# Attention kernel: the top-32 mask added to the scores by GpSimd ahead of the exponential, probabilities and row sums written by ScalarE, one pipeline step more

## The chip, the cores and the metric

The kernel runs on one core of one Trainium2 chip. The metric is the device time of one execution in microseconds (us); lower is better. Five engines work side by side, each through its own queue in program order: TensorE (PE, with its weight loads shown apart as PEld), VectorE (DVE), ScalarE (ACT), GpSimd (POOL) and SyncE (SP, which here only issues transfers). They meet at semaphores.

## The reference

The input is 8 batches of 512 rows of 128 values. A layer of attention is followed by a mixture of experts, a small state-space mixer and the experts again; the change touches the attention alone. Cut to what matters:

```python
qkv = x @ Wqkv.T + bqkv                                 # 16 heads of 64
scores = einsum('bhid,bhjd->bhij', q, k) * SCALE
scores = scores + einsum('bhid,ijd->bhij', q, rel_k_emb[dist])
threshold = top_k(scores, 32)[0][..., -1:]              # the 32nd largest of a row of 512
scores = where(scores < threshold, -inf, scores)
attn = softmax(scores)
for i in range(3):                                      # ORDER = 3
    a_v = attn @ v_curr                                 # i == 0: + attn @ rel_v_emb[dist]
    v_curr = a_v
    res = res + sigmoid(alphas_raw[i]) * v_curr
out = res @ Wout.T + bout
```

## The kernel before, in words

`attention` handles two heads (a pair) of one batch at a time: 64 such iterations (`ITS`), each with 4 tiles of 128 rows (`NT`), so 256 tiles. A tile holds 2 heads x 512 scores on each of 128 partitions. All engines run the same sequence of slots, four in an iteration (`T` = 0 to 3). In one slot an engine works on several tiles of different age: `z.back(2)` is the tile that entered two slots ago, and `z.iteration(-2)` the pair two iterations back. The first and the last iterations are written out and those between are a loop whose body holds two iterations, 8 tiles. What runs when is the order in which `body` names it for each engine; nothing is scheduled automatically.

The way of a tile in the kernel before, all names as in the code:

- slot +0: TensorE makes the relative keys' products; ScalarE spreads them (`rel`), and two transfers through memory shift them into `relj`.
- slot +2: TensorE makes the scores in two banks, and ScalarE copies them into `sc` (a tensor of 2 buffers), three pieces for a head.
- slot +3: VectorE finds the 32 largest of each head's row by four rounds of `max` (8 values each) with `match_replace` between them (L846 to L867). ScalarE negates the row's maximum (`nmax`, L781) and takes the exponential of all 512 scores into `ex` (L788). For head 0 VectorE compares with the 32nd largest, multiplies and sums in one instruction (L875). For head 1 GpSimd compares (L952, into `kept`) and multiplies (L958).
- slot +4: SyncE sends the probabilities' band to memory, TensorE transposes them (L621) and ScalarE copies the transposes into `pt` (L757). ScalarE reads head 1's probabilities once more for their row sum (L825).
- slot +5: the band comes back shifted, ScalarE closes it (`band`, L703 to L716), TensorE turns it (L668), ScalarE keeps it (`band_t`, L797).

Two iterations back, the pair's values are multiplied by the probabilities three times. Each time TensorE multiplies (`mix`, L541), ScalarE copies (`mixed`, L694), TensorE transposes (L600), ScalarE copies (`raw`, L746), and GpSimd divides by the row sums (`u`, L916) and adds into `res` (L925, or L928 and L931). `mix` runs in slots 0, 1 and 2, and the copies and GpSimd's part in slots 1, 2 and 3.

Of the kernel before, what the change touches and what calls it, by code (L numbers as in the profile page):

```python
# [16 lines left out]
P = 128  # L17
B, N, D = 8, 512, 128
NT = N // P
# [9 lines left out]
SCALE = DH ** -0.5  # L29
HALF = MAXREL  # L30
# [354 lines left out]
def attention(nc, sem, sb, ps, k, t):  # L385
# [13 lines left out]
    s.maxes = sem("att_maxes")  # L399
    s.exps = sem("att_exps")  # L400
    s.probs = [sem(f"att_probs_of_head{h}") for h in range(2)]
    s.at_least = sem("att_at_least")
    s.row_sums = sem("att_row_sums")
# [59 lines left out]
    with nc.Block() as block:  # L463
        @block.sync
        def _(sp):
            def body(z, par):
# [14 lines left out]
                d, a = z.back(4), z.back(0)  # L481

                if d:
                    it, Td, n = d
                    qd = Td % 2
                    c0, c1 = known(sp, n + 1, 16 * (it * 2 + Td // 2))
                    for h in range(2):
                        sp.wait_ge(s.probs[h], c0)
# [41 lines left out]
        def _(pe):  # L530
            def body(z, par):
                T = z.T
                old, av, cur, nxt = z.iteration(-3), z.iteration(-2), z.iteration(0), z.iteration(1)
                def mix(it, values):

                    if not early(it * ORDER + T):
                        pe.wait_ge(s.mixed_kept, it * ORDER + T)
                    for jt in range(NT):
                        for h in range(2):
                            lhs = values[:, jt, h * DH:(h + 1) * DH] if T == 0 else values[:, jt, h, :]  # L540
                            last = nc.tensor.matmul(U[h * DH:(h + 1) * DH, :], lhs, pt[par][:, h, jt, :],  # L541
                                                    start=(jt == 0), stop=(jt == NT - 1 and T > 0))
                    return last


# [27 lines left out]
                if old is not None and T == 0:  # L573
                    pe.wait_ge(s.res_chain, old * 5 + 5)
                    if cur is not None:
                        pe.wait_ge(s.k_kept, cur + 1)
# [3 lines left out]
                    last.then_inc(s.res_turned, 1)  # L580

                if av is not None and T > 0:
                    pe.wait_ge(s.mixed_kept, av * ORDER + T)

                    if T == 1 and not early(av):
                        pe.wait_ge(s.out_added, av)
                    if T == 1 and cur is not None:
                        pe.wait_ge(s.k_kept, cur + 1)
                    if T == 2:
                        if cur is not None:  # L590
                            pe.wait_ge(s.v_kept, cur + 1)
                        else:
                            pe.wait_ge(s.raw_kept, av * ORDER + 1)
                    if T == 3:
                        if nxt is not None:
                            pe.wait_ge(s.q_kept, nxt + 1)
                        else:
                            pe.wait_ge(s.raw_kept, av * ORDER + 2)
                    for jt in range(NT):
                        last = nc.tensor.transpose(MISC[:, jt * P:(jt + 1) * P], mixed[:, jt * P:(jt + 1) * P],  # L600
                                                   k.ident[:, :])
                    last.then_inc(s.mixed_turned, 1)

                if av is not None and T == 0:
                    pe.wait_ge(s.probs_kept, (av + 1) * 2 * NT)
                    pe.wait_ge(s.v_ready, av + 1)
                    mix(av, v[par])

                d = z.back(4)
                if d:  # L610
                    it, Td, n = d
                    for h in range(2):
                        pe.wait_ge(s.probs[h], n + 1)
# [12 lines left out]
                if old is not None and T == 0:  # L626
# [7 lines left out]
                if T == 1 and cur is not None:  # L634
                    pe.wait_ge(s.k_kept, cur + 1)
                    if av is not None:
                        pe.wait_ge(s.raw_kept, av * ORDER + 1)
                    for jt in range(NT):
                        last = nc.tensor.matmul(MISC[:, jt * P:(jt + 1) * P], xt[par][:, jt * P:(jt + 1) * P],
                                                pj[par][:, J_WV:J_WV + P], start=True, stop=True)  # L640
                    last.then_inc(s.v_made, 1)

                if T == 2 and nxt is not None:
                    pe.wait_ge(s.pj_in[1 - par], 32 * (z.half(1) + 1))
                    if av is not None:
                        pe.wait_ge(s.raw_kept, av * ORDER + 2)
# [4 lines left out]
                if T == 3 and nxt is not None:  # L651
                    pe.wait_ge(s.q_kept, nxt + 1)
                    if av is not None:
                        pe.wait_ge(s.raw_kept, av * ORDER + 3)
# [3 lines left out]
                e = z.back(5)  # L658
# [12 lines left out]
                if av is not None and T in (1, 2):  # L671
                    pe.wait_ge(s.values_next, av * ORDER + T)
                    last = mix(av, u)
                    last.then_inc(s.mixed, 1)
                if av is not None and T == 0:
# [9 lines left out]
        def _(act):  # L685
            def body(z, par):
                T, sp2 = z.T, z.T % 2
                old, av, cur, nxt = z.iteration(-3), z.iteration(-2), z.iteration(0), z.iteration(1)

                if av is not None and T > 0:  # L690
                    act.wait_ge(s.mixed, av * ORDER + T)
                    if not early(av * ORDER + T - 1):
                        act.wait_ge(s.mixed_turned, av * ORDER + T - 1)
                    nc.scalar.activation(mixed[:, :], U[:, :], ACT.Copy).then_inc(s.mixed_kept, 1)  # L694

                e = z.back(5)
                if e:
# [3 lines left out]
                    act.wait_ge(s.row_sums, n + 1)  # L701
# [17 lines left out]
                if b:  # L719
# [3 lines left out]
                    act.wait_ge(s.rel_kept, n + 1)  # L723
                    for h in range(2):
                        act.wait_ge(s.scores_made, 2 * n + h + 1)
                        if not early(n - 1):
                            act.wait_ge(s.probs[h], n - 1)
                        last = nc.scalar.activation(sc[q][:, h, lo:hi], SC[h][:, lo:hi], ACT.Copy)  # L728
                        if lo > 0:
                            last = nc.scalar.activation(sc[q][:, h, 0:lo], SC[h][:, 0:lo], ACT.Identity,  # L730
                                                        bias=rel[q][:, h, 0:1])
                        if hi < N:
                            last = nc.scalar.activation(sc[q][:, h, hi:N], SC[h][:, hi:N], ACT.Identity,
# [3 lines left out]
                if old is not None and T == 0:  # L737
# [4 lines left out]
                if av is not None and T > 0:  # L742
                    act.wait_ge(s.mixed_turned, av * ORDER + T)
                    if not early(av * ORDER + T - 1):
                        act.wait_ge(s.values_next, av * ORDER + T - 1)
# [3 lines left out]
                d = z.back(4)  # L749
                if d:  # L750
                    it, Td, n = d
                    dpar = 1 - par
# [23 lines left out]
                c = z.back(3)  # L776
                if c:
                    it, Tc, n = c
                    q = Tc % 2
                    act.wait_ge(s.tops, 2 * n + 2)  # L780
                    nc.scalar.activation(nmax[q][:, :], top[q][:, :, 0], ACT.Copy, scale=-1.0).then_inc(s.maxes, 1)  # L781
                    act.wait_ge(s.maxes, n + 1)
                    for h in range(2):
                        if not early(n - 1):
# [1146 lines left out]
```

## Time and profile before

| what | value |
|---|---|
| median of 3 runs | 3345.88 us (3342.76 to 3358.94) |
| span of the profiled execution, first to last instruction | 3382.6 us |
| VectorE (DVE) busy | 2933.7 us, 87% |
| TensorE (PE) busy | 2884.2 us, 85% |
| ScalarE (ACT) busy | 2463.6 us, 73% |
| GpSimd (POOL) busy | 1642.2 us, 49% |

The profile is of one execution. The only time that it gives for that execution is its span, 3382.6 us, 36.7 us or 1.1% over the median of the timed runs. Shares are of the whole span, of which attention's tiles fill about 69 us to 2660 us.

### The profile page before, as it was taken

The numbers are of one execution on the slowest core, as the hardware profiler recorded it, in microseconds if no ns is written. First come the engines' busy times: TensorE is split into PE (matmuls) and PEld (weight loads), VectorE is DVE, ScalarE is ACT, GpSimd is POOL, SyncE is SP. The second block draws the span as 40 slices with busy tenths as digits, with TensorE's granted clock in tenths as the row PEclk, the third lists the DMA queues.
The fourth block names the chain that finished last, engine by engine and source line by source line (L and its number), as shares of the span: only waits on it lengthen the run. The fifth ranks groups of instructions, "written<-read, shape, count | busy, mean of one in ns | idle before, by whom it ended". The sixth has DMA issues, their size and how long they took to land. (4 is left out here: it accounts for less than half of the span.)

```text
span 3382.6 us, 62340 instructions
## 1 busy us (share of the span) xinstructions
PE 2884.2 (85%) x13152; PEld 1671.5 (49%) x13152; DVE 2933.7 (87%) x6964; ACT 2463.6 (73%) x7615; POOL 1642.2 (49%) x1196
## 2 busy tenths in 40 slices
PE   4799889998889889988888998898888677888958
PEld 2454444454444445444444444444444344677743
DVE  5999999999999999999999999999999556676546
ACT  3888888888888888888888888888888523332214
POOL 1455555555555555555555555555555424222104
PEclk7999999999999999999999999999999867677659
DMA  4444444444444444444444444444444100000001
GB/s 124 135 133 126 136 130 130 130 132 126 132 129 136 127 134 129 130 134 132 132 132 130 132 132 134 132 134 126 134 130 127 48 17 10 16 7 4 0 7 45
DMA packets 293411, 356.42 MB, mean 105 GB/s; under 512 B 24850, under 2 KB 239956, under 8 KB 293204
## 3 DMA queue, kind: packets, MB, share of 16 engines
q1 hardware_dynamic: 291076, 351.66, 35.3%
q10 hardware_dynamic: 2128, 2.85, 0.3%
q14 instruction: 182, 1.49, 0.1%
q8 instruction: 25, 0.41, 0.1%
HBM read 140.00 MB, written 169.87 MB: 92 GB/s over the span
## 5 line engine op out<-in xcount | busy, mean ns | idle before, releaser
L855 DVE MAX8 top<-work 128x8 f32<-128x512 f32 x1536 | 978.5, 677 | 0.0
L952 POOL TENSOR_SCALAR kept<-scores,top 128x512 f32<-128x512 f32 x256 | 489.9, 1914 | 540.0 <-DVE top L855 535.5
L865 DVE MATCH_REPLACE8 work<-top,work 128x512 f32<-128x512 f32 x1024 | 682.7, 673 | 0.0
L556 PE MATMUL bank<-keys_of_head,qt 128*128 128x512 f32 x1024 | 598.2, 669 | 0.0
L541 PE MATMUL bank<-probs_t,u 128*64 128x512 f32 x2048 | 467.7, 599 | 4.0 <-POOL u L916 3.6
L852 DVE MAX8 top<-scores 128x8 f32<-128x512 f32 x512 | 327.4, 679 | 99.8 <-issue 83.9
L916 POOL TENSOR_TENSOR u<-raw,inverse 128x512 f32<-128x512 f32 x192 | 200.2, 1043 | 433.1 <-ACT raw L746 433.1
L958 POOL TENSOR_TENSOR probs_of_tile<-kept,exps 128x512 f32<-128x512 f32 x256 | 326.6, 1276 | 61.1 <-POOL kept L952 53.7
L560 PEld LDWEIGHTS bank<-relj,identity 128*128 128x128 f32 x1024 | 210.4, 206 | 285.7 <-issue 276.9
L788 ACT ACTIVATE exps<-scores,nmax 128x512 f32<-128x512 f32 x512 | 341.7, 714 | 8.3
L865 DVE MATCH_REPLACE8 work<-top,scores 128x512 f32<-128x512 f32 x512 | 341.3, 673 | 0.0
L621 PE MATMUL bank<-identity,probs_of_tile 128*128 128x128 f32 x2048 | 280.3, 276 | 25.7 <-POOL probs_of_tile L958 20.4
L560 PE MATMUL bank<-relj,identity 128*128 128x256 f32 (+1 forms) x1024 | 291.2, 368 | 7.2 <-DMA relj<-rel_scratch 7.2
L757 ACT ACTIVATE probs_t<-bank 128x512 f32<-128x512 f32 x512 | 284.1, 626 | 1.6 <-PE bank L621 1.6
L728 ACT ACTIVATE scores<-bank 128x192 f32<-128x192 f32 (+1 forms) x512 | 180.7, 353 | 132.8 <-POOL probs_of_tile L958 88.9
L621 PEld LDWEIGHTS bank<-identity,probs_of_tile 128*128 128x128 f32 x2048 | 227.9, 141 | 89.6 <-issue 63.7
L556 PEld LDWEIGHTS bank<-keys_of_head,qt 128*128 128x128 f32 x1024 | 186.8, 206 | 169.8 <-issue 163.3
L541 PEld LDWEIGHTS bank<-probs_t,u 128*64 128x64 f32 x2048 | 135.7, 137 | 245.0 <-issue 220.4
L875 DVE SCALAR_TENSOR_TENSOR probs_of_tile<-scores,top,exps 128x512 f32<-128x512 f32 x256 | 233.5, 912 | 9.5 <-DVE top L855 4.7
L541 PE MATMUL bank<-probs_t,v 128*64 128x512 f32 x1024 | 235.4, 602 | 0.0
L703 ACT ACTIVATE band<-band 128x129 f32<-128x129 f32 x512 | 155.5, 304 | 100.3 <-DMA band<-probs_scratch 96.0
L694 ACT ACTIVATE mixed<-bank 128x512 f32<-128x512 f32 x192 | 114.6, 597 | 116.3 <-PE bank L541 68.4
(259 smaller groups left out, 5594.2 us busy)
## 6 DMA issues: line engine op xcount, KB each, us to landing
rel_scratch<-rel SPq DMA_DIRECT2D x256, 383.0 KB, 3.8
relj<-rel_scratch SPq DMA_DIRECT2D x256, 256.0 KB, 2.8
probs_scratch<-probs_of_tile SPq DMA_DIRECT2D x256, 256.0 KB, 2.5
band<-probs_scratch SPq DMA_DIRECT2D x256, 256.0 KB, 3.6
pair_j<-table_j SPq DMA_DIRECT2D x64, 257.0 KB, 2.9
xt<-stream_normed_t SPq DMA_DIRECT2D x64, 256.0 KB, 3.0
pair_o<-table_o SPq DMA_DIRECT2D x64, 67.0 KB, 2.4
experts_xs<-stream_normed_t SPq DMA_DIRECT2D x16, 256.0 KB, 2.3
```

What stands on the lines that cost most here:

```text
L541: last = nc.tensor.matmul(U[h * DH:(h + 1) * DH, :], lhs, pt[par][:, h, jt, :], start=(jt == 0), stop=(jt == NT - 1 and T > 0))
L556: nc.tensor.matmul(SC[h][:, :], qt[bpar][:, Tb * P:(Tb + 1) * P], t.kz[bpar][h][:, :], start=True, stop=False)
L560: nc.tensor.matmul(SC[h][:, lo:hi], k.ident[:, :], relj[q][:, h, at:at + hi - lo], start=False, stop=True).then_inc(s.scores_made, 1)
L621: last = nc.tensor.transpose(PT[h][:, jt * P:(jt + 1) * P], t.prob[Td][:, h, HALF + jt * P:HALF + (jt + 1) * P], k.ident[:, :])
L757: nc.scalar.activation(pt[dpar][:, h, :, Td * P:(Td + 1) * P], PT[h][:, :].rearrange("p (j i) -> p j i", j=NT), ACT.Copy).then_inc(s.probs ...
L788: nc.scalar.activation(ex[q][:, h, :], sc[q][:, h, :], ACT.Exp, bias=nmax[q][:, h:h + 1]).then_inc(s.exps, 1)
L852: nc.vector.max(top[q][:, h, 0:8], sc[q][:, h, :]).then_inc(s.tops, 1)
L855: nc.vector.max(top[q][:, h, 8 * r:8 * r + 8], work[:, h, :]).then_inc(s.next_tops, 1)
L865: nc.vector.match_replace(out=work[:, h, :], in_to_replace=top[q][:, h, 8 * r:8 * r + 8], in_values=sc[q][:, h, :] if r == 0 else work[:, ...
L875: nc.vector.scalar_tensor_tensor(out=t.prob[Tc][:, 0, HALF:HALF + N], in0=sc[q][:, 0, :], scalar=top[q][:, 0, TOPK - 1:TOPK], in1=ex[q][:, ...
L952: nc.gpsimd.tensor_scalar(kept[:, :], sc[q][:, 1, :], top[q][:, 1, TOPK - 1:TOPK], None, ALU.is_ge).then_inc(s.at_least, 1)
L958: nc.gpsimd.tensor_tensor(t.prob[Tc][:, 1, HALF:HALF + N], kept[:, :], ex[q][:, 1, :], ALU.mult).then_inc(s.probs[1], 1)
```

## The change: what it does

1. GpSimd gets the whole mask. For each tile it negates the maximum and the 32nd value of both heads in one small instruction (`neg`), and then, for each of the two heads: adds minus the 32nd value and multiplies by 2^100 (one instruction), takes the minimum with 0 and the maximum with -3e38 (one instruction; so 0 for a score that stays and a huge negative value for one that goes), and adds this to the scores in place.
2. ScalarE's exponential reads the masked scores, writes the probabilities themselves, and sums each row with the same instruction. `nmax`, `ex`, `kept`, VectorE's L875, GpSimd's L952 and L958 and ScalarE's L781 and L825 are gone.
3. The exponential moves to slot +4. The probabilities' transfer and transposes move to slot +5, the band to slot +6. The three multiplications of the values move to slots 1, 2 and 3, the third one's copies to slot 0 of the next iteration, the values' projection `v` from slot 1 to slot 0, and the output's projection from slot 0 to slot 1.
4. The scores have 4 buffers, in place of 2.

The core of the diff:

```diff
-    sc = two("scores", [P, 2, N])
+    sc = [sb(f"scores{T}", [P, 2, N]) for T in range(NT)]
...
-    nmax = two("nmax", [P, 2])
-    ex = two("exps", [P, 2, N])
-    kept = sb("kept", [P, N])
+    neg = two("minus_max_and_least", [P, 2, 2])
+    cut = sb("cut", [P, 2, N])
...
+                    if not early(n - 3):
+                        act.wait_ge(s.probs, 2 * n - 6)
                     for h in range(2):
                         act.wait_ge(s.scores_made, 2 * n + h + 1)
-                        if not early(n - 1):
-                            act.wait_ge(s.probs[h], n - 1)
...
-                c = z.back(3)
-                if c:
-                    it, Tc, n = c
-                    q = Tc % 2
-                    act.wait_ge(s.tops, 2 * n + 2)
-                    nc.scalar.activation(nmax[q][:, :], top[q][:, :, 0], ACT.Copy, scale=-1.0).then_inc(s.maxes, 1)
...
+                x = z.back(4)
+                if x:
+                    it, Tx, n = x
+                    xpar, q = 1 - par, Tx % 2
...
+                        act.wait_ge(s.masked, 2 * n + h + 1)
+                        nc.scalar.activation(t.prob[Tx][:, h, HALF:HALF + N], sc[Tx][:, h, :], ACT.Exp,
+                                             bias=neg[q][:, h, 0:1],
+                                             accum_out=rs[xpar][:, 2 * Tx + h:2 * Tx + h + 1]).then_inc(s.probs, 1)
...
-                    act.wait_ge(s.probs[1], n + 1)
-                    nc.scalar.activation(ex[Td % 2][:, 1, :], t.prob[Td][:, 1, HALF:HALF + N], ACT.Copy,
-                                         accum_out=rs[dpar][:, 2 * Td + 1:2 * Td + 2]).then_inc(s.row_sums, 1)
...
+                    if not early(n - 1):
+                        dve.wait_ge(s.negated, n - 1)
...
-                    nc.vector.scalar_tensor_tensor(out=t.prob[Tc][:, 0, HALF:HALF + N], in0=sc[q][:, 0, :],
-                                                   scalar=top[q][:, 0, TOPK - 1:TOPK], in1=ex[q][:, 0, :],
-                                                   op0=ALU.is_ge, op1=ALU.mult,
-                                                   accum_out=rs[cpar][:, 2 * Tc:2 * Tc + 1]).then_inc(s.probs[0], 1)
...
-                    nc.gpsimd.tensor_scalar(kept[:, :], sc[q][:, 1, :], top[q][:, 1, TOPK - 1:TOPK], None,
-                                            ALU.is_ge).then_inc(s.at_least, 1)
...
-                    nc.gpsimd.tensor_tensor(t.prob[Tc][:, 1, HALF:HALF + N], kept[:, :], ex[q][:, 1, :],
-                                            ALU.mult).then_inc(s.probs[1], 1)
+                    nc.gpsimd.tensor_scalar(neg[q][:, :, :], ends, -1.0, 0.0, ALU.mult, ALU.add).then_inc(s.negated, 1)
...
+                    for h in range(2):
+                        nc.gpsimd.tensor_scalar(cut[:, h, :], sc[Tc][:, h, :], neg[q][:, h, 1:2], STEEP,
+                                                ALU.add, ALU.mult).then_inc(s.compared, 1)
...
+                        nc.gpsimd.tensor_scalar(cut[:, h, :], cut[:, h, :], 0.0, NEG,
+                                                ALU.min, ALU.max).then_inc(s.cut, 1)
...
+                        nc.gpsimd.tensor_tensor(sc[Tc][:, h, :], sc[Tc][:, h, :], cut[:, h, :],
+                                                ALU.add).then_inc(s.masked, 1)
```

What this does to the order of GpSimd's instructions, in the loop's body. First a slot 2 of the kernel before: `u`, `tmp` and `res` are the values' part, `kept` and `probs_of_tile` the mask of head 1. (REGISTER_ALU and ISA rows work out what a semaphore is compared with.)

```order
L909 REGISTER_ALU
L915 REGISTER_ALU
L916 TENSOR_TENSOR u<-raw,inverse 128x512
L928 TENSOR_TENSOR tmp<-u,pair_o 128x512
L930 REGISTER_ALU
L931 TENSOR_TENSOR res<-res,tmp 128x512
L365 ISA
L952 TENSOR_SCALAR kept<-scores,top 128x512
L954 REGISTER_ALU
L955 ISA
L958 TENSOR_TENSOR probs_of_tile<-kept,exps 128x512
```

The same work after the change, now in slot 3: the mask is seven instructions of both heads, six of them over 512 values on each partition.

```order
L893 REGISTER_ALU
L899 REGISTER_ALU
L900 TENSOR_TENSOR u<-raw,inverse 128x512
L912 TENSOR_TENSOR tmp<-u,pair_o 128x512
L914 REGISTER_ALU
L915 TENSOR_TENSOR res<-res,tmp 128x512
L366 ISA x2
L940 TENSOR_SCALAR minus_max_and_least<-top 128x4
L946 TENSOR_SCALAR cut<-scores,minus_max_and_least 128x512 x2
L951 TENSOR_SCALAR cut<-cut 128x512 x2
L955 TENSOR_TENSOR scores<-scores,cut 128x512 x2
```

What moved: the two instructions of the mask became seven, and the part with `u` stands ahead of them as before.

## Rows read from the trace of the kernel before

**Rows 1.** Busy time of each engine in two stretches of attention.

```profile
core 0: us, PE busy (x) PEld busy (x) DVE busy (x) ACT busy (x) POOL busy (x), PEclk, DMA share, GB/s
300.00:2500.00 2200.00, 1961.83 (x9100) 1067.66 (x9102) 2113.50 (x4877) 1909.03 (x6016) 1238.23 (x923) 0.97 0.45 131
```

**Rows 2.** Waits of VectorE from 300 to 2500 us: total, times, longest.

```profile
DVE top L852 <- issue: 80.7, 27, 3.5
DVE probs_of_tile L875 <- DVE top L855: 2.8, 17, 0.2
```

**Rows 3.** Timeline of VectorE, one loop body of 8 tiles: start, us, engine.

```profile
1015.19 1.29 DVE L852 MAX8 top<-scores 128x8 f32<-128x512 f32 x2 [3.03 <-issue]
...
1023.92 0.73 DVE L875 SCALAR_TENSOR_TENSOR probs_of_tile<-scores,top,exps 128x512 f32<-128x512 f32 x1
...
1025.25 1.27 DVE L852 MAX8 top<-scores 128x8 f32<-128x512 f32 x2
...
1082.07 1.49 DVE L875 SCALAR_TENSOR_TENSOR probs_of_tile<-scores,top,exps 128x512 f32<-128x512 f32 x1 [0.17 <-DVE top L855]
...
1083.49 1.28 DVE L852 MAX8 top<-scores 128x8 f32<-128x512 f32 x2
...
1096.89 0.69 DVE L852 MAX8 top<-scores 128x8 f32<-128x512 f32 x1 [3.37 <-issue]
```

**Rows 4.** Groups of VectorE: count, busy us, mean ns.

```profile
L875 DVE SCALAR_TENSOR_TENSOR probs_of_tile<-scores,top,exps 128x512 f32<-128x512 f32 x256 | 233.5, 912 | 9.5 <-DVE top L855 4.7 <-ACT exps L788 3.0
```

**Rows 5.** Groups of GpSimd, shapes kept apart.

```profile
L952 POOL TENSOR_SCALAR kept<-scores,top 128x512 f32<-128x512 f32 x256 | 489.9, 1914 | 540.0 <-DVE top L855 535.5 <-issue 4.0
L958 POOL TENSOR_TENSOR probs_of_tile<-kept,exps 128x512 f32<-128x512 f32 x256 | 326.6, 1276 | 61.1 <-POOL kept L952 53.7 <-ACT band L712 5.4
L916 POOL TENSOR_TENSOR u<-raw,inverse 128x512 f32<-128x512 f32 x192 | 200.2, 1043 | 433.1 <-ACT raw L746 433.1
L931 POOL TENSOR_TENSOR res<-res,tmp 128x512 f32<-128x512 f32 x128 | 163.3, 1276 | 10.0
...
L938 POOL TENSOR_TENSOR v<-vraw,pair_j 128x512 f32<-128x512 f32 x64 | 83.7, 1308 | 131.1 <-ACT vraw L805 131.1
...
L220 POOL MEMSET zeros<- 128x256 f32 x1 | 0.3, 312 | 0.3 <-POOLq L1920 0.3
L226 POOL TENSOR_SCALAR_AFFINE_SELECT anti_identity<-anti_identity 128x128 f32<-128x128 f32 x1 | 0.3, 293 | 0.0
...
L221 POOL MEMSET identity<- 128x128 f32 x1 | 0.2, 205 | 0.0
```

**Rows 6.** Timeline of GpSimd around one tile's mask and the values' part.

```profile
1073.68 1.28 POOL L938 TENSOR_TENSOR v<-vraw,pair_j 128x512 f32<-128x512 f32 x1 [1.76 <-ACT vraw L805]
1074.93 1.56 POOL L952 TENSOR_SCALAR kept<-scores,top 128x512 f32<-128x512 f32 x1
1076.74 1.27 POOL L958 TENSOR_TENSOR probs_of_tile<-kept,exps 128x512 f32<-128x512 f32 x1 [0.24 <-POOL kept L952]
1079.50 1.04 POOL L916 TENSOR_TENSOR u<-raw,inverse 128x512 f32<-128x512 f32 x1 [1.49 <-ACT raw L746]
1080.62 1.04 POOL L928 TENSOR_TENSOR tmp<-u,pair_o 128x512 f32<-128x512 f32 x1
1081.74 1.27 POOL L931 TENSOR_TENSOR res<-res,tmp 128x512 f32<-128x512 f32 x1
1082.99 2.00 POOL L952 TENSOR_SCALAR kept<-scores,top 128x512 f32<-128x512 f32 x1
```

**Rows 7.** Groups of ScalarE, 300 to 2500 us.

```profile
L825 ACT ACTIVATE exps<-probs_of_tile 128x512 f32<-128x512 f32 x216 | 134.8, 624 | 1.3
...
L825 ACT ACTIVATION_READ_ACCUMULATOR exps<-probs_of_tile 128x1 f32 x216 | 41.5, 192 | 0.0
...
L781 ACT ACTIVATE nmax<-top 128x2 f32<-128x2 f32 x217 | 60.3, 278 | 0.0
```

**Rows 8.** Timeline, all engines: the values' chain from one multiplication to the next.

```profile
1030.35 3.65 PE L541 MATMUL bank<-probs_t,u 128*64 128x512 f32 x16
...
1034.06 0.60 ACT L694 ACTIVATE mixed<-bank 128x512 f32<-128x512 f32 x1 [0.51 <-PE bank L541]
...
1037.88 0.33 ACT L728 ACTIVATE scores<-bank 128x192 f32<-128x192 f32 x1 [0.89 <-POOL probs_of_tile L958]
...
1038.51 0.60 ACT L746 ACTIVATE raw<-bank 128x512 f32<-128x512 f32 x1
...
1039.27 1.04 POOL L916 TENSOR_TENSOR u<-raw,inverse 128x512 f32<-128x512 f32 x1 [1.49 <-ACT raw L746]
...
1040.50 1.08 PE L541 MATMUL bank<-probs_t,u 128*64 128x512 f32 x4
```

**Rows 9.** Waits of TensorE and ScalarE from 300 to 2500 us.

```profile
PE bank L678 <- ACT band_t L797: 111.6, 54, 2.1
...
ACT scores L728 <- POOL probs_of_tile L958: 81.0, 81, 2.0
```

More of the change, by code:

```diff
@@ L29 @@
 SCALE = DH ** -0.5
+STEEP = 2.0 ** 100
 HALF = MAXREL
@@ L398, in attention @@
     s.tops = sem("att_tops")
[L399 to L403, printed above, removed]
+    s.negated = sem("att_negated")
+    s.compared = sem("att_compared")
+    s.cut = sem("att_cut")
+    s.masked = sem("att_masked")
+    s.probs = sem("att_probs")
     s.probs_turned = sem("att_probs_turned")
@@ L624, in body @@
                         last.then_inc(s.probs_turned, 1)
-                if old is not None and T == 0:
+                if T == 0 and cur is not None:
+                    pe.wait_ge(s.k_kept, cur + 1)
+                    if old is not None:
+                        pe.wait_ge(s.raw_kept, old * ORDER + 3)
+                    for jt in range(NT):
+                        last = nc.tensor.matmul(MISC[:, jt * P:(jt + 1) * P], xt[par][:, jt * P:(jt + 1) * P],
+                                                pj[par][:, J_WV:J_WV + P], start=True, stop=True)
+                    last.then_inc(s.v_made, 1)
+                if T == 1 and old is not None:
                     pe.wait_ge(s.res_kept, old + 1)
@@ L632, in body @@
                     last.then_inc(s.out_made, 1)
[L634 to L641, printed above, removed]
                 if T == 2 and nxt is not None:
@@ L669, in body @@
                     last.then_inc(s.band_turned, 1)
[L671 to L675, printed above, removed]
+                if av is not None and T in (2, 3):
+                    pe.wait_ge(s.values_next, av * ORDER + T - 1)
+                    mix(av, T - 1, u).then_inc(s.mixed, 1)
+                if av is not None and T == 1:
                     pe.wait_ge(s.band_kept, (av + 1) * NT)
@@ L688, in body @@
                 old, av, cur, nxt = z.iteration(-3), z.iteration(-2), z.iteration(0), z.iteration(1)
[L690 to L693, printed above, removed]
+                turning, step = (old, 3) if T == 0 else (av, T - 1)
+                if turning is not None and step > 0:
+                    act.wait_ge(s.mixed, turning * ORDER + step)
+                    if not early(turning * ORDER + step - 1):
+                        act.wait_ge(s.mixed_turned, turning * ORDER + step - 1)
                     nc.scalar.activation(mixed[:, :], U[:, :], ACT.Copy).then_inc(s.mixed_kept, 1)
-                e = z.back(5)
+                e = z.back(6)
                 if e:
@@ L885, in body @@
                     nc.vector.reciprocal(inv[par][:, :], rs[par][:, :]).then_inc(s.inverse, 1)
-                if old is not None and T == 0:
+                if old is not None and T == 1:
                     dve.wait_ge(s.out_made, old + 1)
@@ L952, in body @@
[L952 to L959 removed]
+                        pool.wait_ge(s.probs, used)
@@ new lines, in body @@
+                    ends = bass.AP(top[q][:, :, :].tensor, top[q][:, :, :].offset,
+                                   [list(top[q][:, :, :].ap[0]), [TOPK, 2], [TOPK - 1, 2]])
+                    nc.gpsimd.tensor_scalar(neg[q][:, :, :], ends, -1.0, 0.0, ALU.mult, ALU.add).then_inc(s.negated, 1)
+                    met()
+                    pool.wait_ge(s.negated, turned_over)
+                    if not early(before):
+                        pool.wait_ge(s.masked, before)
+                    for h in range(2):
+                        nc.gpsimd.tensor_scalar(cut[:, h, :], sc[Tc][:, h, :], neg[q][:, h, 1:2], STEEP,
+                                                ALU.add, ALU.mult).then_inc(s.compared, 1)
```

180 lines of the change are left out of this document (84 added, 96 removed).

## The prediction

> **What bounds the kernel now.** I read the windows first. From 300 to 2500 us, all attention, VectorE is busy 2113.5 of 2200 us, 96%; TensorE 89%, ScalarE 87%, GpSimd 56% [rows 1]. The next view is who VectorE waits for: almost nobody. Its idle time is 80.7 us in 27 pieces put down to "issue" [rows 2]. The timeline shows one such piece at each turn of the loop, 3.03 and 3.37 us, between the last tile of one body and the first of the next [rows 3]. So VectorE sets the pace: one body of 8 tiles lasts 1096.89 - 1015.19 = 81.70 us [rows 3], 10.21 us a tile, 40.85 us an iteration. The whole of attention is 64 iterations of that.
>
> In that body a tile's search takes 8.73 us (1015.19 to 1023.92) [rows 3], and behind it comes L875, the masked product for head 0. L875 has two prices. It lasts 0.73 us at 1023.92 and 1.49 us at 1082.07 [rows 3], where GpSimd was adding into `res` (1081.74 to 1083.01) when it began [rows 6]. Its mean is 912 ns over 256 [rows 4]. The two exclude each other for a while. After the change VectorE's per-tile work is `max` and `match_replace` alone; two `max` take 1.27 to 1.29 us wherever they stand [rows 3], also at 1083.49, beside L952 on GpSimd [rows 6]. So I charge no contention.
>
> **The change on VectorE.** It loses L875: 256 x 0.912 = 233 us [rows 4], and in the sampled body the 7 us that are left of its 81.70 when what VectorE keeps is taken off. It keeps the search (8 x 8.74), the reciprocal and the add into the stream of each iteration (1025.25 - 1023.92 = 1.33 us less L875's 0.66 [rows 3], so 0.67 twice), and the 3.3 us at the loop's turn: 69.9 + 1.3 + 3.3 = 74.6 us, 37.3 an iteration. Its new wait, for `negated` two tiles back, has a whole tile's slack; behind it stands only its own next search. If VectorE stays the bound the gain is (40.85 - 37.3) x 64 = 227 us.
>
> **The change on ScalarE.** Per tile it loses L781 (0.28 us) and L825 (0.62 us and an accumulator read of 0.19, which overlaps its neighbours) and gains two accumulator reads of 0.19 at most [rows 7]: 0.5 to 0.7 us less a tile. From 8.8 us busy a tile (1909 us over 2200 at 10.14 us a tile [rows 1]) it falls to about 8.2, under VectorE's 9.3. The four score buffers take away its wait for the mask of the tile two back, 81.0 us in 81 waits [rows 9].
>
> **TensorE** does the same work in another order. What paces it is a chain: `mix` starts at 1030.35, ScalarE copies at 1034.06, copies `raw` at 1038.51 after a wait of 0.89 us for the score buffer, GpSimd makes `u` at 1039.27, and the next `mix` starts at 1040.50 [rows 8]. That is 10.15 us for a slot, and 9.26 without the 0.89. Two slots of an iteration have it. The other two take 40.85 - 2 x 10.15 = 20.55 us today, with a stall of 2.1 us at L678 in them, 54 times [rows 9]; I take 1.2 us off, since less ScalarE work will stand ahead of `band_t`, and get 19.3. This estimate from those rows gives 2 x 9.3 + 19.3 = 37.9, with some jitter 38.3 us an iteration. It lies a little over VectorE's 37.3. The one step more is one slot at the end: +5 to +9 us once.
>
> **The change on GpSimd**, which decides. The part that it keeps costs, from starts in the timeline: `u`, `tmp`, `res` 1079.50 to 1082.99 = 3.49 us, twice an iteration; `u` with the first `res` 2.3; `v` 1073.68 to 1074.93 = 1.25 [rows 6]. Sum 10.6 us an iteration. It loses the mask of head 1, and gains for each tile:
> - one small negation and a handover to itself: 0.1 plus 0.24 (the gap at 1076.74 [rows 6]);
> - two adds of two tensors: 2 x 1.27 = 2.55 (the same form as L958 and L931, 1276 ns [rows 5]);
> - four `tensor_scalar` over 512 values with arithmetic, each x plus 0.08 of gap (1080.62 + 1.04 to 1081.74 [rows 6]).
>
> That is 3.2 + 4x a tile, so 23.5 + 16x an iteration, and at most 1.5 more if a turn of the loop costs GpSimd the 3 us that it costs VectorE. For x = 0.77 this gives 35.8 to 37.3; it ties with VectorE at x = 0.86 (0.77 with the turn), and with today's 40.85 at x = 1.08 (0.99).
>
> No row shows x: the trace has no arithmetic `tensor_scalar` on GpSimd. Bounds: below, a memset. 256 columns take 312 ns and 128 take 205 [rows 5], 0.84 ns a column, so 512 take 0.53 us. Above, L952, one comparison over 512 values. Its mean is 1914 ns [rows 5], but it starts beside L875 nearly always; where it doesn't, at 1074.93, it takes 1.56 us [rows 6]. Between: two-input products where one input is a broadcast take 1.04 us (L916 and L928), which read one tensor more than a `tensor_scalar`; and the affine select of 128 columns takes 293 ns, which with the fixed part of the memset (205 - 107 = 98 ns) is 1.5 ns a column, 0.88 us for 512. A comparison must make a 0 or a 1 of a condition and is the dearest of these per value; a two-tensor product is below it at 1.27 us though it reads twice. I take x = 0.8, by the affine select and a little under the broadcast product, with 0.53 to 1.56 as its range.
>
> Two rules of the Trainium skill, "GPSIMD Engine Reference", stand beside this. Section 3.1 has a tight loop over 512 elements at 769 ns, and says that bodies which produce a condition cost about twice those that don't; by that x would be 0.77 and an iteration of GpSimd 35.8 us. Against the change speaks section 4.1: elementwise work belongs on VectorE, GpSimd being about twice as slow with two inputs. The trace agrees with the second as far as it shows it (1.27 us against L875's 0.73).
>
> With x = 0.8 GpSimd needs 36.3 to 37.8 us an iteration, TensorE's chain 38.3, VectorE 37.3. Three engines within 2 us of each other seldom meet the best of them, so I take 38.5: (38.5 - 40.85) x 64 = -150 us, +6 for the extra slot. Against the profiled 3382.6 that is 3239; the median of the runs stands 36.7 below that span, and taken off it the forecast is **3202 us**. Its own range is 3115 to 3320: VectorE's bound with nothing lost (-227), up to x = 1.0.
>
> **Rivals.**
> 1. GpSimd becomes the bound at a price like the broadcast product with two operations, x about 1.05 to 1.3. An iteration is then 40.3 to 44.3 us and up to 1.5 more: 0 to +315 us, centre +130, 3480 us. For it: two operations in an instruction, and nothing in the trace that shows the second to be free. The rule of section 4.1 above, taken for one input too, would end here. Against: the affine select. It ends slower, and decides from x = 1.08 on. Chance 0.22.
> 2. All arithmetic costs like the comparison, x = 1.43 to 1.56: 46.4 to 48.5 us an iteration, and 1.5 more with the turn: +355 to +585, about 3815 us. For it: the only `tensor_scalar` in the trace over 512 values. Against: it alone has a condition. Chance 0.15.
> 3. The mask is cheap, but the values' chain or the waits at L678 keep the old pace: `mix` to `mix` stays at 10.15 us because ScalarE's order, not the buffer, fixes `raw`. Then 40.85 us an iteration, within 20 us of before. Against: 0.89 us of it is plainly the score buffer [rows 8]. Chance 0.07.
>
> The forecast keeps 0.56.
>
> **How the numbers follow.** A change of 0.5%, 17 us, is about what a measurement of this kernel can tell from none. Faster: the forecast's 0.56 and a little of rival 1's and 3's lower edges, 0.58. Same: 0.08. Slower: 0.34. The range runs from 3115 (VectorE's own bound) to 3600, x about 1.28: above it lies rival 2 and the tail of rival 1, some 0.17.
>
> **What the profile after would show.** `cut` rows on GpSimd near 0.8 us each (rival 1: over 1.05; rival 2: 1.4 and more). No L875, and VectorE's `max` waiting a little for ScalarE's scores or for `negated` instead of never. ScalarE without waits for the score buffer. `mix` to `mix` in two slots near 9.3 us. If x is right and the time is not, look for ScalarE waiting at the exponential for `masked`, and TensorE at the band. If GpSimd is the bound, it is busy over 95%, and VectorE waits for `negated`.

## The result, and the profile after

The changed kernel takes 3400.6 us (median of 4 runs, 3399.5 to 3404.1), the kernel before 3348.5 us beside it. The ratio is 1.017, 95% interval 1.014 to 1.020: slower by 52 us, where the prediction said 3202 us and faster. The page of the changed kernel, its span, busy times and clock:

```profile
span 3398.5 us, 62039 instructions
...
PE 2871.5 (84%) x13152; PEld 1666.5 (49%) x13152; DVE 2738.2 (81%) x6452; ACT 2286.3 (67%) x7359; POOL 2167.6 (64%) x2476
...
PEclk7999999999999999999999999999999968676659
```

VectorE lost 195 us of work and ScalarE 177, and GpSimd gained 525. So the work went where it was meant to go, and no engine is full: in attention VectorE fell from 96% busy [rows 1] to 88% (1934.5 of 2200 us in the row below), GpSimd is at 76%. The same stretch of the changed kernel:

```profile
300.00:2500.00 2200.00, 1942.85 (x9037) 1064.15 (x9037) 1934.49 (x4412) 1742.83 (x5747) 1669.90 (x1991) 0.96 0.44 130
```

How long an iteration lasts on the average is read from VectorE's reciprocal, once an iteration: the first and the last start, divided by 63. Before and after:

```profile
L885 DVE RECIPROCAL inverse<-row_sums x64: 189/197/203, 126.9 to 2666.2; 128x8 f32<-128x8 f32 x64
```

```profile
L862 DVE RECIPROCAL inverse<-row_sums x64: 176/183/203, 122.0 to 2683.8; 128x8 f32<-128x8 f32 x64
```

That is 40.31 us before and 40.66 after. What took the place of VectorE's work is in the waits of the changed kernel from 300 to 2500 us (total, times, longest):

```profile
POOL v L922 <- PE bank L676: 270.4, 53, 5.7
...
DVE stream L869 <- PE bank L638: 180.6, 53, 4.0
POOL u L900 <- ACT raw L744: 143.7, 108, 3.1
ACT band L701 <- DMA band<-probs_scratch: 137.3, 126, 2.5
...
PE bank L676 <- ACT band_t L794: 107.0, 53, 2.0
PE bank L541 <- POOL u L900: 91.5, 54, 2.6
```

The rows of `v`, of `stream` and the last are new: in the kernel before, `v` waited for ScalarE's copy (92.9 us in the same stretch), VectorE's addition into `stream` did not wait, and TensorE waited 3.6 us for `u` in the whole span. The output's products and the addition that reads them both moved from slot 0 to slot 1; why the addition now waits 3.4 us an iteration was not taken apart, but the experiments below tell whether it sets the pace. The last row can be followed in the timeline of all engines, one iteration's slots 1 and 2:

```profile
990.38 1.08 PE L676 MATMUL bank<-band_t,rel_values 128*64 128x512 f32 x4 [2.02 <-ACT band_t L794]
...
991.55 1.27 POOL L922 TENSOR_TENSOR v<-vraw,pair_j 128x512 f32<-128x512 f32 x1 [4.70 <-PE bank L676]
...
992.90 0.20 POOL L940 TENSOR_SCALAR minus_max_and_least<-top 128x4 f32<-128x4 f32 x1
...
994.93 0.60 ACT L744 ACTIVATE raw<-bank 128x512 f32<-128x512 f32 x1
995.98 2.51 POOL L955 TENSOR_TENSOR scores<-scores,cut 128x512 f32<-128x512 f32 x2
...
998.44 1.05 POOL L900 TENSOR_TENSOR u<-raw,inverse 128x512 f32<-128x512 f32 x1
...
999.54 5.35 PE L541 MATMUL bank<-probs_t,u 128*64 128x512 f32 x16 [2.56 <-POOL u L900]
```

GpSimd is about to write `v` for the next pair. The buffer is the one that `mix` of step 0 reads, and its release is the semaphore `mixed`, which TensorE raises only after L676, the last product of slot 1. Before the change that product stood in slot 0, a slot ahead of `v`; now both are in slot 1. GpSimd waits 4.70 us, with slot 1's mask and slot 2's `u` queued behind. `raw` is there at 995.53 (994.93 + 0.60), but `u` starts at 998.44, and TensorE waits 2.56 us. What that wait costs on top is seen in L541: 5.35 us for 16 products, where before it was 3.65 [rows 8]. The granted clock goes with it. Two windows of the changed kernel at that place: behind each stretch's length stand the busy times of TensorE, its weight loads, VectorE, ScalarE and GpSimd, then the granted clock:

```profile
996.00:999.50 3.50, 0.99 (x4) 0.28 (x2) 3.50 (x7) 3.12 (x10) 3.49 (x4) 1.00 0.41 116
...
1001.00:1003.00 2.00, 2.00 (x8) 0.53 (x6) 2.00 (x6) 0.00 (x0) 1.77 (x3) 0.50 0.23 41
```

TensorE was busy for 0.99 of the 3.5 us from 996 to 999.5, at full clock (2.4 GHz). From 1001 to 1003 us it was busy all the time, at 0.50, the lower of its two levels (1.2 GHz).

This is the longer of two kinds of iteration that take turns. From 300 to 2500 us TensorE waited 26 times for about 2.55 us and 28 times for 0.9 to 1.2 us, and 21 of the 26 long waits were followed by 16 products in 5.0 to 5.35 us. Nor is the lower level new. The kernel before shows it too, here behind a stall of 2.06 us at L678 that ended at 1021.69:

```profile
1023.00:1026.00 3.00, 3.00 (x6) 1.45 (x6) 3.00 (x8) 2.10 (x9) 1.84 (x1) 0.50 0.40 110
```

The means from 300 to 2500 us are 0.97 before [rows 1] and 0.96 after, so the lower level by itself does not explain the loss.

GpSimd's prices, the unknown of the prediction, came out on its cheap side. Groups of GpSimd in the changed kernel:

```profile
L955 POOL TENSOR_TENSOR scores<-scores,cut 128x512 f32<-128x512 f32 x512 | 643.4, 1279 | 0.0
L946 POOL TENSOR_SCALAR cut<-scores,minus_max_and_least 128x512 f32<-128x512 f32 x512 | 354.3, 692 | 65.3 <-issue 40.8 <-POOL minus_max_and_least L940 0.2
L951 POOL TENSOR_SCALAR cut<-cut 128x512 f32<-128x512 f32 x512 | 305.8, 613 | 21.5
```

### The profile page after: what moved, and what is told of

Its sections match the earlier page's. It is cut to its first block and busy times, and to the rows that moved or that the text cites. A ratio compares the mean times of both kernels' runs of the same rounds, so it can differ in the third digit from the quotient of the medians.

```text
span 3398.5 us, 62039 instructions
## 1 busy us (share of the span) xinstructions
PE 2871.5 (84%) x13152; PEld 1666.5 (49%) x13152; DVE 2738.2 (81%) x6452; ACT 2286.3 (67%) x7359; POOL 2167.6 (64%) x2476
## 5 line engine op out<-in xcount | busy, mean ns | idle before, releaser
L955 POOL TENSOR_TENSOR scores<-scores,cut 128x512 f32<-128x512 f32 x512 | 643.4, 1279 | 0.0
L541 PE MATMUL bank<-probs_t,u 128*64 128x512 f32 x2048 | 508.4, 642 | 112.6 <-POOL u L900 112.5
L841 DVE MAX8 top<-scores 128x8 f32<-128x512 f32 x512 | 339.6, 684 | 112.5 <-ACT scores L731 101.9
L946 POOL TENSOR_SCALAR cut<-scores,minus_max_and_least 128x512 f32<-128x512 f32 x512 | 354.3, 692 | 65.3 <-issue 40.8
L784 ACT ACTIVATE probs_of_tile<-scores,minus_max_and_least 128x512 f32<-128x512 f32 x512 | 378.6, 773 | 21.8 <-POOL scores L955 21.2
L541 PEld LDWEIGHTS bank<-probs_t,u 128*64 128x64 f32 x2048 | 145.7, 147 | 388.5 <-issue 250.2
L951 POOL TENSOR_SCALAR cut<-cut 128x512 f32<-128x512 f32 x512 | 305.8, 613 | 21.5
L922 POOL TENSOR_TENSOR v<-vraw,pair_j 128x512 f32<-128x512 f32 x64 | 81.3, 1270 | 336.6 <-PE bank L676 315.6
L620 PE MATMUL bank<-identity,probs_of_tile 128*128 128x128 f32 x2048 | 270.0, 275 | 8.3 <-ACT probs_of_tile L784 4.4
L869 DVE TENSOR_TENSOR stream<-bank,stream 128x512 f32 (+1 forms) x64 | 44.3, 692 | 253.0 <-PE bank L638 253.0
```

The source lines that it names most:

```text
L620: last = nc.tensor.transpose(PT[h][:, jt * P:(jt + 1) * P], t.prob[Td][:, h, HALF + jt * P:HALF + (jt + 1) * P], k.ident[:, :])
L784: nc.scalar.activation(t.prob[Tx][:, h, HALF:HALF + N], sc[Tx][:, h, :], ACT.Exp, bias=neg[q][:, h, 0:1], accum_out=rs[xpar][:, 2 * Tx + h ...
L841: nc.vector.max(top[q][:, h, 0:8], sc[Tc][:, h, :]).then_inc(s.tops, 1)
L946: nc.gpsimd.tensor_scalar(cut[:, h, :], sc[Tc][:, h, :], neg[q][:, h, 1:2], STEEP, ALU.add, ALU.mult).then_inc(s.compared, 1)
L951: nc.gpsimd.tensor_scalar(cut[:, h, :], cut[:, h, :], 0.0, NEG, ALU.min, ALU.max).then_inc(s.cut, 1)
L955: nc.gpsimd.tensor_tensor(sc[Tc][:, h, :], sc[Tc][:, h, :], cut[:, h, :], ALU.add).then_inc(s.masked, 1)
```

## The experiments

All times are medians with the ratio to the kernel before, run on the same chip, since the kernel before itself lies between 3342 and 3359 us from chip to chip. Differences to the changed kernel are of medians and carry that spread: the first four gains below are 107, 111, 90 and 173 us so, and 129, 123, 108 and 193 us by the ratios. Theory 1 is the new wait just told. Its rivals are that GpSimd's amount of work, or VectorE's, or the longer pipeline holds the kernel.

**v behind the mask.** In GpSimd's body the block of `v` moves from ahead of the mask to behind it.

```diff
-                if T == 1 and cur is not None:
-                    pool.wait_ge(s.v_kept, cur + 1)
...
                         nc.gpsimd.tensor_tensor(sc[Tc][:, h, :], sc[Tc][:, h, :], cut[:, h, :],
                                                 ALU.add).then_inc(s.masked, 1)
+                if T == 1 and cur is not None:
+                    pool.wait_ge(s.v_kept, cur + 1)
```

> The changed kernel, with GpSimd's addition for the values of the next pair (v) moved behind the mask of the same slot; nothing else. Theory 1 (the new wait): in the changed kernel v waits 5.1 us once an iteration for the end of the multiplication by the old v (L676), the mask and u stand behind it, TensorE then waits 2.6 us for u and runs the next products at a lower clock. Then this edit gives back 2 to 3 us an iteration, 130 to 200 us: 3200 to 3270 us, and the wait at L541 for u falls from 91 us (300 to 2500 us) to under 20. Rival (GpSimd's added work itself, or the longer pipeline): the wait is only where slack shows, and the time stays within 0.5% of 3400 us.

Measured: 3293.8 us, ratio 0.979 (0.974 to 0.983). 107 us come back from this order alone, short of the 130 to 200 that were expected. The row of TensorE's wait for `u`, 91.5 us in the changed kernel, is gone from its waits; of the weight loads' wait for it 17.9 us are left in 107 waits.

**v released by its own semaphore.** `v` stays ahead of the mask.

```diff
-                    mix(av, 0, v[par])
+                    mix(av, 0, v[par]).then_inc(s.v_read, 1)
...
-                    if not early((cur - 2) * ORDER + 1):
-                        pool.wait_ge(s.mixed, (cur - 2) * ORDER + 1)
+                    if not early(cur - 1):
+                        pool.wait_ge(s.v_read, cur - 1)
```

> The changed kernel, v left ahead of the mask, but released by a semaphore of its own when the first multiplication (which is all that reads v) has ended, instead of by the end of L676. Theory 1: as the run before, 3200 to 3270 us, since the multiplication ends at 1027.7 us in the trace and GpSimd is free at 1028.8. If the order on GpSimd matters and not the wait, this one stays at 3400 us while the run before gains.

Measured: 3289.4 us, ratio 0.980 (0.976 to 0.985), the same as the run before, and 19 us short of the expected range as well: what matters is that `v` does not hold up what stands behind it, not where it stands. The timeline of this kernel shows `v` right behind the mask of slot 0, without a wait, four microseconds before the start of the product that it used to wait for:

```profile
1025.00 1.28 POOL L923 TENSOR_TENSOR v<-vraw,pair_j 128x512 f32<-128x512 f32 x1
...
1028.99 1.08 PE L677 MATMUL bank<-band_t,rel_values 128*64 128x512 f32 x4 [2.02 <-ACT band_t L795]
...
1034.58 1.04 POOL L901 TENSOR_TENSOR u<-raw,inverse 128x512 f32<-128x512 f32 x1 [2.62 <-ACT raw L745]
...
1035.81 3.65 PE L542 MATMUL bank<-probs_t,u 128*64 128x512 f32 x16
```

Now GpSimd waits for `raw`, and the next `mix` starts 0.19 us after `u` has ended and takes 3.65 us at full clock. The stall of 2.02 us at L677 (L676 of the changed kernel) stands unchanged.

**The band's copy first.** In slot 1 ScalarE's L794 goes ahead of the two exponentials.

```diff
+                if e and T == 1:
+                    it, Te, n = e
...
+                                         ACT.Copy).then_inc(s.band_kept, 1)
                 x = z.back(4)
                 if x:
...
-                if e:
+                if e and T != 1:
```

> The changed kernel, with ScalarE's copy of the band (L794) in slot 1 moved ahead of the two exponentials of that slot. The wait of TensorE at L676 (2.0 us, once an iteration) should fall to about 0.6 and v be released 1.4 us earlier. Theory 1: TensorE's stalls set the pace, so 1.4 to 3 us an iteration, 3210 to 3310 us. Rival: no change, within 0.5% of 3400 us.

Measured: 3310.9 us, ratio 0.985 (0.981 to 0.988), 90 us faster than the changed kernel and 1 us outside the slow edge of what was expected. Two waits of this kernel, from 300 to 2400 us:

```profile
POOL v L932 <- PE bank L676: 194.9, 52, 4.2
...
PE bank L676 <- ACT band_t L780: 32.0, 52, 0.6
```

TensorE's stall fell from 2.0 to 0.6 us, and GpSimd's wait for `v` from 5.1 to 3.7, by the same 1.4.

**Both edits** (own semaphore, band's copy first).

> Both edits: v released by its own semaphore, and the band's copy ahead of the exponentials in slot 1. Theory 1: TensorE then needs about 36 us an iteration and VectorE's 37.3 is the bound: 3180 to 3210 us. Rival: 3400 us, or no better than the better of the two single edits because another engine holds at 38 us.

Measured: 3227.6 us, ratio 0.960 (0.956 to 0.963). This is 173 us under the changed kernel and 4% under the kernel before; the single edits gave 111 and 90. It is not quite the 3180 to 3210 that VectorE's bound would have given. The longer pipeline is all in this kernel, so it is not what made the changed kernel slow. The page and the windows (300 to 2400 us; 1.00 is the granted clock):

```profile
span 3230.6 us, 62097 instructions
...
PE 2795.1 (87%) x13152; PEld 1635.6 (51%) x13152; DVE 2715.0 (84%) x6452; ACT 2260.0 (70%) x7359; POOL 2167.0 (67%) x2476
```

```profile
300.00:2400.00 2100.00, 1917.28 (x9251) 1059.96 (x9250) 1959.20 (x4513) 1763.09 (x5895) 1708.58 (x2037) 1.00 0.47 140
```

The clock went from 0.96 to 1.00 with no edit to TensorE's work: in this stretch the mean rounds to full clock. Each repair by itself gave 0.97 and 0.98. An iteration lasts 38.0 us by VectorE's reciprocal, of which VectorE is busy 35.5 (1959.2 / 2100 of it). Its waits show what is next:

```profile
ACT band L702 <- DMA band<-probs_scratch: 243.0, 179, 2.7
...
DVE stream L880 <- PE bank L639: 139.5, 55, 3.4
```

**The kernel before, band's copy first.** The same edit to the kernel before, in slot 0.

```diff
+                if e and T == 0:
...
                 c = z.back(3)
                 if c:
...
-                if e:
+                if e and T != 0:
```

> The kernel before, with the same edit to it as gave 90 us in the changed one: ScalarE's copy of the band (L797) in slot 0 ahead of that slot's exponentials. Theory 1: before was held by VectorE, so taking 1.4 us of TensorE's stall away buys nothing, within 0.5% of the kernel before. Rival (TensorE's stalls held the kernel before as well): 60 to 120 us faster.

Measured: 3341.2 against 3341.6 us, ratio 0.999 (0.997 to 1.001). What is worth 90 us in the changed kernel is worth nothing in the kernel before, though the same stall fell from 2.1 us [rows 9] to 0.6 (32.1 us in 52 waits). In part another wait took its place: TensorE's waits for GpSimd's probabilities at L621 grew from 10 to 34 us (300 to 2500 us).

**Less work for VectorE**, in the kernel before and in the changed one. The last round of the search reads half a row, so the threshold of both is another one.

```diff
-                                nc.vector.max(top[q][:, h, 8 * r:8 * r + 8], work[:, h, :]).then_inc(s.next_tops, 1)
+                                nc.vector.max(top[q][:, h, 8 * r:8 * r + 8], work[:, h, 0:N // 2 if r == 3 else N]).then_inc(s.next_tops, 1)
```

> The kernel before, with the last round of the search (values 25 to 32) looking at the first 256 of 512 scores only, so its threshold is another one: 0.55 to 0.7 us less VectorE work a tile, with every wait kept. Theory 1 (VectorE is the bound of the kernel before): 120 to 175 us faster. If TensorE's chain is the true bound: under 40 us.

> The changed kernel with the same shorter last round. Theory 1 (VectorE no longer sets the pace there): within 1% of 3400 us, at most 35 us faster. If VectorE still is the bound: 120 to 175 us faster.

Measured: the kernel before 3327.1 us, ratio 0.996 (0.992 to 0.999); the changed kernel 3398.7 us, ratio 1.018 (1.015 to 1.021), against 1.017 without the edit. The second is as expected: VectorE has no part in the changed kernel's time. The first misses theory 1 and falls where its rival stood, under 40 us. Two of these `max` take 0.54 us less a tile together (409 against 676 ns each), 138 us in all, and 14 came out. The groups of VectorE's L875 show one place where the rest went, and the waits another:

```profile
L875 DVE SCALAR_TENSOR_TENSOR probs_of_tile<-scores,top,exps 128x512 f32<-128x512 f32 x256 | 271.1, 1059 | 61.3 <-ACT exps L788 35.9 <-DVE top L855 21.6 <-issue 2.4
```

L875 grew from 912 to 1059 ns [rows 4], 38 us in all. It now lies beside GpSimd's instructions for longer, 0.94 us of overlap on the average against 0.74, and 96 of the 256 take over 1.2 us against 55. Its wait for ScalarE's exponential grew from 3.0 to 35.9 us. So VectorE in the kernel before was busy 96% of the time and still did not hold it alone; something else, which these two runs do not name, was only some 14 us behind.

**Both in the kernel before**, band's copy first and the shorter round.

> The kernel before with both of its single edits: ScalarE's band copy first in slot 0, and the shorter last round of VectorE's search. Alone each gave under 0.5%. Theory 2 (two bounds that lie within 15 us of each other, VectorE's work and TensorE's chain with its stall): together they give clearly more than the sum, 50 to 120 us faster than the kernel before. Rival (a third chain holds it, such as the score buffers): again under 20 us.

Measured: 3322.5 us, ratio 0.989 (0.987 to 0.991), 36 us. That is twice the sum of the two (0.1% and 0.4%), but neither the 50 us of theory 2 nor under the 20 of its rival. TensorE's stall is a part of the second bound and not the whole. What else holds it wasn't settled; ScalarE still waits for the score buffers there (66.6 us in 68 waits). The kernel before with four score buffers was not tried.

**Less work for GpSimd.** The two clamping instructions of a tile are left out, and the factor is 1, so that the mask is no mask; first in the changed kernel.

```diff
-STEEP = 2.0 ** 100
+STEEP = 1.0
...
-                        nc.gpsimd.tensor_scalar(cut[:, h, :], cut[:, h, :], 0.0, NEG,
-                                                ALU.min, ALU.max).then_inc(s.cut, 1)
```

> The changed kernel with GpSimd's two clamping instructions of each tile left out (and the factor 2^100 set to 1, so the mask is no mask): 1.2 us less GpSimd work a tile. Theory 1: GpSimd's amount of work is not the bound, but in slot 1 its mask stands between v and u, so u comes 1.2 us sooner once an iteration and a part of the 2.6 us at L541 goes: 1.2 to 2 us an iteration, 75 to 130 us faster. Rival (GpSimd's load is the bound): 4 x 1.2 us an iteration, 300 us, down to what the next engine allows at 37.3 us an iteration, 3190 us. Rival (it has no part in it): no change.

Measured: 3297.8 us, ratio 0.987 (0.984 to 0.989), 103 us faster than the changed kernel. This is inside what theory 1 gave, but by itself it would also suit a weaker form of the rival. Its waits from 300 to 2500 us are those of theory 1. GpSimd did not use the time that it saved but waited longer for `v`, and TensorE's wait for `u` went from 91.5 us to 16.9 (total, times, longest):

```profile
POOL v L922 <- PE bank L676: 384.4, 55, 7.8
...
PE bank L541 <- POOL u L900: 16.9, 21, 1.1
```

The same edit on top of both repairs tells them apart:

> The kernel with both edits, and GpSimd's two clamping instructions of each tile left out (factor 1 in place of 2^100, so the mask is no mask). In the changed kernel leaving them out gave 100 us. Theory 1: that was the mask standing between the late v and u, so with v released in time it gives nothing, within 0.5% of 3228 us. Rival (GpSimd's amount of work is a bound in its own right): 50 us or more faster.

Measured: 3223.2 us, ratio 0.963 (0.961 to 0.965), against 0.960 for both repairs alone. 1.2 us less a tile on GpSimd is worth 100 us while the late `v` pushes the mask in front of `u`, and nothing when it doesn't. GpSimd's amount of work is no bound in either kernel: in the changed one it stands idle before `v`, and in the repaired one less of it changes nothing.

**What holds the repaired kernel.** Two more on top of both repairs. In one VectorE's addition into the stream, which waits for TensorE's output products, moves behind the first round of slot 2's tile:

```diff
-                if old is not None and T == 1:
-                    dve.wait_ge(s.out_made, old + 1)
...
+                        if T == 2 and r == 0:
+                            into_stream()
```

> The kernel with both edits (v's own semaphore, the band's copy first in slot 1), and VectorE's addition into the stream moved from behind slot 1's tile to behind the first round of slot 2's tile. VectorE waits there 2.5 to 3.4 us once an iteration for the output's products. If VectorE's 37.3 us are the bound of that kernel (38.0 us an iteration), this gives 10 to 40 us. If TensorE's and ScalarE's chain holds it, no change within 0.5% of 3228 us.

> The kernel with both edits and the shorter last round of VectorE's search. If VectorE is the bound of that kernel at 3228 us, 100 us or more faster; if TensorE's and ScalarE's chain is, within 0.5% of it; between, both are near.

Measured: 3217.3 us, ratio 0.957 (0.955 to 0.959), for the first, and 3223.2 us, ratio 0.959 (0.956 to 0.961), for the second. Neither is told apart from 0.960 (0.956 to 0.963). The first says little by itself, since 10 us faster is both the low end of what VectorE's bound would give and inside the 0.5%. In it the wait for the output's products is gone, and VectorE waits for ScalarE's scores in its place (104 us from 300 to 2400 us). The second decides, where 100 us or more would have come: VectorE is not the bound at 38.0 us an iteration either. By what is left that is the chain through ScalarE, TensorE and the band's transfer; it was not tested by itself.

## Why the prediction was wrong, step by step

**GpSimd's price, "I take x = 0.8": right in kind, about a fifth too dear.** The arithmetic instructions take 0.69 and 0.61 us, less than half of the comparison's 1.56 [rows 6]. The affine select and the broadcast product, the nearest rows, both lay over it. One mask takes 5.6 us (1000.69 to 1006.29 in the trace of the changed kernel), where 3.2 + 4 x 0.8 = 6.4 was forecast. Rivals 1 and 2 fall with that: the kernel became slower without either of them. Of the Trainium skill, "GPSIMD Engine Reference", the 769 ns of section 3.1 for a tight loop over 512 values was nearer than 0.8 and still over both measured prices. The rule on bodies that produce a condition stands in its section 7 and not in 3.1; here the comparison costs 2.3 to 2.5 times the arithmetic. The row of section 4.1 that the prediction quotes calls only operations with two inputs twice as slow, and those with one input roughly line-rate; 0.69 and 0.61 us, beside 0.64 for VectorE's `max` over as many values [rows 3], agree, so that row spoke against rival 1 and not for it.

**What VectorE and ScalarE lose: right.** VectorE's busy time fell by 195 us (L875's 233 us are gone, and the rest grew a little), and ScalarE's by 0.7 us a tile (177 us / 256), as stated. No contention was forecast for `max` and `match_replace`, and `match_replace` takes 675 ns after as 673 before, `max` 679 as 677.

**The step that failed stands under the change on GpSimd: "the part that it keeps costs ... `v` 1.25".** It was charged as work and never as a wait. The prediction went through the waits that the diff adds (`negated`, `masked`), but not through those whose text is the same and whose other end has moved. The line `pool.wait_ge(s.mixed, (cur - 2) * ORDER + 1)` is in both kernels. TensorE's signal for it moved from slot 0 to slot 1, and `v` stayed in slot 1. The runs showed in its place a wait of 5.1 us once an iteration (270.4 us in 53 waits), and behind it TensorE's for the late `u` (91.5 us in 54 waits). The two runs on `v` show what it costs: 107 and 111 us.

**The values' chain, "9.26 without the 0.89": too short, because a wait took the place of the one removed.** In the kernel with `v` repaired, `mix` to `mix` is 1045.78 - 1035.81 = 9.97 us, with both repairs 9.80. ScalarE no longer waits for a score buffer, but from 300 to 2400 us it waits longer for the band's transfer: 70.1 us in 139 waits before, 243.0 in 179 with both repairs. That this is what holds `raw` back is argued from the order of ScalarE's work and was not tested. This is rival 3 in part. "Two slots of an iteration have it" was misread as well. Of the three intervals between the starts of an iteration's multiplications only the one from step 1 to step 2 is like that (medians from 300 to 2400 us before: 16.6, 10.15 and 14.2); with both repairs they are 15.0, 9.8 and 13.0, so most of what was gained lies in the other two.

**"I take 1.2 us off" the stall at L678: wrong.** It stayed at 2.0 us (107.0 us in 53 waits). ScalarE's copy still stood behind both exponentials, and taking `nmax` away did not bring it forward. Moving it did, and was worth 62 us with `v` repaired (3289 to 3228).

**"VectorE sets the pace": half right.** Shortening its work by 138 us in the kernel before gave 14. A second bound lay close behind, which the busy share of 96% can't show. Its 37.3 us for the time after were too many as well. The 3.3 us at the loop's turn are no row in the waits of the changed or the repaired kernel, and VectorE is busy only 35.5 us an iteration there; why they are gone was not tested.

**The baseline, "(38.5 - 40.85) x 64 = -150 us": some 55 us too much.** The sampled body of 40.85 us was longer than the mean of its own trace, 40.31: 35 us. And that execution was a long one. Taking 36.7 off brings the sum to the median of the runs, but the gain that it is added to was still counted against the long execution. The kernel before with the band's copy first, which takes as long as the kernel before (ratio 0.999), has 39.98 us an iteration in a trace of 3344.0 us: 21 us more. Against 39.98 the same working gives -95 us and a forecast near 3257 us, an estimate. By spans the change costs 16 us, by medians 52.

**Small slips.** GpSimd's kept part adds to 10.5 us, not 10.6; L875 is put in with 0.66 us where its row has 0.73; the lower end of the range, 3382.6 - 227 - 36.7, is 3119, not 3115. None of them moves the forecast.

Together: of the 198 us between 3202 and 3400.6, the late `v` is 111 and the stall at L676 62, when they are repaired in this order (90 for the stall's repair and 83 for the other, in the reverse order). The 26 that are left come close to the baseline, some 55 us too low, less the 31 us by which 38.0 us an iteration is under the forecast's 38.5. So with both waits gone the forecast's pace was met and a little more, but its parts were not the ones named.

## What to carry to other kernels

When a stage moves by a slot, list every semaphore that it raises, and look at who waits for it, also in lines that the diff leaves alone: a signal that moves later is a new wait for an unchanged line. A buffer is best released by the instruction that last reads it, not by a later signal that happens to exist; here that one line was worth 3.3%. And a busy share of 96% shows that an engine has no slack, not that the kernel gets shorter with its work: to know what the next bound allows, shorten it in an experiment first.

## What the runs showed of the hardware that was not expected

- On GpSimd, over 128 x 512 values: add and multiply with one scalar for each partition 0.69 us, minimum and maximum with constants 0.61 us, a product of two tensors 1.28 us. One comparison took 1.56 us in the 29 of 256 cases in the kernel before where VectorE's L875 did not run beside it, and 1.96 us on the average where it did. Two arithmetic operations in one instruction cost less than half of one comparison alone.
- A wait of TensorE can cost more than its length. After 2.56 us of waiting in the changed kernel, 16 products took 5.35 us in place of 3.65, with a granted clock of 0.50 from 1001 to 1003 us. Of 26 such waits from 300 to 2500 us, 21 were followed by slower products and 5 by 3.65 us. Another wait for `u`, of 0.89 us at 1041.89, was followed by 3.65 us at full clock, and after the 27 others of its kind, of 0.9 to 1.2 us, they took 3.65 us as well. With both repairs TensorE waits 0.6 us for the band's copy and up to 2.1 us for `raw` (66.6 us in 55 waits), and the mean granted clock from 300 to 2400 us is 1.00. In the changed kernel with the band's copy first, 26 of 105 such multiplications (300 to 2400 us) took over 4.5 us, though only 4 of the 26 stood right behind a wait of over 1.5 us. So the length of a single wait did not tell in these runs whether the clock fell; what does was not tested.
